# Token means and variances scaled on ScalarE instead of VectorE, with two steps of VectorE's order exchanged

## The reference, cut to what matters

```python
def _ln_c(v, eps=1e-06):          # over the 64 channels
    m = jnp.mean(v, axis=1, keepdims=True)
    s = jnp.var(v, axis=1, keepdims=True)
    return (v - m) / jnp.sqrt(s + eps)
...
# x is (4, 64, 128, 128)
x = x + window_attention(_ln_c(x))          # windows of 8x8, 4 heads of 16, with a position bias
t = _to_tokens(x)
# _ln_t: mean and variance over the last axis, eps 1e-5
t = t + moe(_ln_t(t))
x = _from_tokens(t, x)
...
def moe(x):
    router_probs = softmax(x @ router_w + router_b)      # 8 experts
    top_p, top_i = top_k(router_probs, 2)
    top_p = top_p / sum(top_p)
    expert_out = einsum('bnd,edc->bnec', x, expert_w) + expert_b
    return sum over the two of top_p * gathered expert_out
```

## Time and profile before

| | us |
|---|---|
| median of 3 runs | 1341.95 (1341.09 to 1342.88) |
| the profiled execution's own time | 1341.82 |
| its span, first to last instruction | 1340.0 |
| TensorE busy | 1237.9 (92%) |
| VectorE busy | 1138.4 (85%) |
| GpSimd busy | 918.0 (69%) |
| ScalarE busy | 875.7 (65%) |

### The profile page before, as it was taken

How to read it: one execution, slowest core, us unless ns; L and a number is a source line. 1 busy time by engine, 2 the same in 40 slices (tenths; PEclk the granted TensorE clock), 3 DMA queues, 4 the chain that set the end, 5 groups by cost and what they waited for, 6 DMA issues and landing times.

```text
span 1340.0 us, 47446 instructions
## 1 busy us (share of the span) xinstructions
PE 1237.9 (92%) x19840; PEld 781.4 (58%) x19840; DVE 1138.4 (85%) x2436; ACT 875.7 (65%) x1615; POOL 918.0 (69%) x809
## 2 busy tenths in 40 slices
PE   4579999999999999999999999999999999999986
PEld 3456666656666665665566566566566665666542
DVE  5548998998898899899888889989888888888865
ACT  5357677667666767767666777776667666666632
POOL 6456777777666777777766777876866667666642
PEclk8579999999999999999999999999999999999988
DMA  7012332322223233232222323322222222222221
GB/s 199 1 34 60 90 90 67 90 58 53 58 66 75 67 90 90 67 75 58 54 64 58 90 73 84 90 67 59 58 67 51 60 66 59 64 55 59 59 66 40
DMA packets 95554, 91.53 MB, mean 68 GB/s; under 512 B 26797, under 2 KB 62253, under 8 KB 95342
## 3 DMA queue, kind: packets, MB, share of 16 engines
q1 hardware_dynamic: 95342, 88.49, 27.0%
HBM read 36.03 MB, written 17.83 MB: 40 GB/s over the span
## 4 chain that ended last, share of the span: by engine, by line
PE 50%; DVE 23%; ACT 10%; issue 8%; POOL 7%; DMA 1%; SPq 1%; POOLq 0%; DVEq 0%; ACTq 0%
PE bank_y L523 10%; PE bank_s L407 8%; PE bank_s L381 6%; DVE t_g L950 6%; PE bank_t L422 5%; PE bank_o L435 4%; DVE mx L842 4%; DVE x L864 4%; PE bank_p L450 3%; PE bank_e L479 3%; ACT k_m L644 3%; PE bank_g L512 2%; DVE o_t L855 2%; ACT prob_t L668 2%; PE bank_e L472 2%
## 5 line engine op out<-in xcount | busy, mean ns | idle before, releaser
L1069 POOL TENSOR_TENSOR prob<-prob,mx 128x512 f32<-128x512 f32 x256 | 261.7, 1044 | 88.5 <-DVE mx L842 87.8
L523 PE MATMUL bank_y<-t_g,w_exp 128*64 128x512 f32 x1024 | 279.2, 622 | 16.7 <-DVE t_g L950 12.5
L664 ACT ACTIVATE prob<-prob 128x512 f32<-128x512 f32 x256 | 160.7, 628 | 147.4 <-POOL prob L1069 145.7
L1091 POOL TENSOR_TENSOR t_g<-t_t,g_copy 128x512 f32<-128x512 f32 x128 | 165.4, 1292 | 125.5 <-ACT g_copy L696 125.2
L668 ACT ACTIVATE prob_t<-bank_t 128x512 f32<-128x512 f32 x256 | 152.4, 595 | 135.8 <-PE bank_t L422 135.7
L1081 POOL TENSOR_TENSOR ln<-ln,mhalf 128x8 f32<-128x8 f32 x64 | 105.1, 1642 | 158.1 <-DVE ln L878 158.1
L835 DVE TENSOR_TENSOR prob<-bank_s,rel 128x1024 f32<-128x1024 f32 x128 | 156.6, 1223 | 39.7 <-PE bank_s L407 35.1
L422 PEld LDWEIGHTS bank_t<-idn,prob 128*128 128x128 f32 x1024 | 111.1, 144 | 130.2 <-issue 105.4
L422 PE MATMUL bank_t<-idn,prob 128*128 128x128 f32 x1024 | 169.1, 288 | 12.7 <-ACT prob_t L668 10.6
L950 DVE TENSOR_TENSOR t_g<-t_t,bank_p 128x512 f32<-128x512 f32 x256 | 174.3, 681 | 7.3 <-PE bank_p L512 6.9
L407 PEld LDWEIGHTS bank_s<-k_m,q_t 32*64 32x64 f32 x4096 | 114.0, 135 | 72.2 <-issue 68.6
(11 more groups left out here) (114 smaller groups left out, 2400.3 us busy)
## 6 DMA issues: line engine op xcount, KB each, us to landing
t_t<-t_rout SPq DMA_DIRECT2D x256, 128.0 KB, 2.4
x_in<-in_x SPq DMA_DIRECT2D x68, 256.0 KB, 3.3
r_b<-recip_rows SPq DMA_DIRECT2D x64, 256.0 KB
out_y<-y_out SPq DMA_DIRECT2D x128, 128.0 KB, 2.5
r_in<-sum_b SPq DMA_DIRECT2D x64, 16.0 KB
recip_rows<-r_out SPq DMA_DIRECT2D x64, 16.0 KB, 1.4
gate_sel<-in_sel SPq DMA_DIRECT2D x1, 512.0 KB
rel<-in_relb SPq DMA_DIRECT2D x1, 256.0 KB
```

Source lines behind the costliest of these rows:

```text
L523: mm(B_Y[C * a:C * a + C, :], w_exp[:, pair, :], t_g[:, (2 * pair + a) % TG, :], start=False, stop=(pair == MIXES // 2 - 1), skip_group_ch ...
L664: A(prob[:, i], prob[:, i], ACT.Exp).then_inc(p_ready.sem, 1)
L1069: G.tensor_tensor(sc, sc, mx[:, i, :].unsqueeze(2).broadcast_to([P, 2 * HEADS, NTOK]), ALU.subtract).then_inc(s_shifted.sem, 1)
L1091: G.tensor_tensor(t_g[:, u % TG, :], t_t[:, p, u % 2, :], g_copy[:, n % 2, :], ALU.mult).then_inc(tg_pool.sem, 1)
```

## The change

- The division of the token sums by 64 (L872) and the scaling of the summed squares with the epsilon (L878) leave VectorE. ScalarE does them as `Copy` with scale and bias, in two new functions `token_mean` and `token_variance`. They wait for VectorE's sums (`lsum`, `lvar`), and GpSimd now waits for them (`mean_ready`, `var_ready`). VectorE's sums go to rows 0 and 4 of `ln` in SBUF instead of to columns of the PSUM bank B_E.
- In ScalarE's slot `token_variance(j-2)` stands right behind `square(j-2)`, ahead of `copy_sums`; `token_mean(j-1)` stands between `exps(j+1, 0)` and `spread_values`.
- In VectorE's slot the second `maxima` goes ahead of `reciprocals` and of the statistics' steps (`reciprocals` ahead of two of them), and gate 7 ahead of `add_input`.

```diff
-        ln = sb("ln", [P, 4, ROWS])
+        ln = sb("ln", [P, 5, ROWS])
...
+            def token_mean(g):
+                act.wait_ge(lsum.sem, lsum.at(g, 1))
+                A(ln[:, 1, :], ln[:, 0, :], ACT.Copy, scale=1.0 / C).then_inc(mean_ready.sem, 1)
+
+            def token_variance(g):
+                act.wait_ge(lvar.sem, lvar.at(g, 1))
+                A(ln[:, 2, :], ln[:, 4, :], ACT.Copy, scale=1.0 / C, bias=LN_T_EPS).then_inc(var_ready.sem, 1)
...
# ScalarE's slot
                 if routing_on:
                     square(j - 2)
+                    token_variance(j - 2)
                 if outputting:
                     copy_sums(j - 1)
...
                 if projecting:
                     exps(j + 1, 0)
+                if outputting:
+                    token_mean(j - 1)
+                if projecting:
                     spread_values(j + 1, 1 - p)
                     exps(j + 1, 1)
...
# VectorE
             def token_mean(g, p):
                 dve.wait_ge(x2_ready.sem, x2_ready.at(g, 1))
-                V.tensor_reduce(B_E[:, LN_AT:LN_AT + ROWS], x2[:, p], AX.X, ALU.add).then_inc(lsum.sem, 1)
-                dve.wait_ge(lsum.sem, lsum.at(g, 1))
-                V.tensor_scalar(ln[:, 1, :], B_E[:, LN_AT:LN_AT + ROWS], 1.0 / C, None, ALU.mult).then_inc(lsum.sem, 1)
+                V.tensor_reduce(ln[:, 0, :], x2[:, p], AX.X, ALU.add).then_inc(lsum.sem, 1)
...
-                V.tensor_reduce(B_E[:, LN_AT + ROWS:LN_AT + 2 * ROWS], xc2[:, :, :], AX.X, ALU.add).then_inc(lvar.sem, 1)
-                dve.wait_ge(lvar.sem, lvar.at(g, 1))
-                V.tensor_scalar(ln[:, 2, :], B_E[:, LN_AT + ROWS:LN_AT + 2 * ROWS], 1.0 / C, LN_T_EPS, ALU.mult,
-                                ALU.add).then_inc(lvar.sem, 1)
+                V.tensor_reduce(ln[:, 4, :], xc2[:, :, :], AX.X, ALU.add).then_inc(lvar.sem, 1)
...
# VectorE's slot
                 if mixing:
                     routing(j - 3, 15, 19)
+                if attending:
+                    maxima(j, 1)
                 if work.step == SQUARES:
                     total_squares(work.batch)
+                if outputting:
+                    reciprocals(j - 1)
                 if work.step == PLANES:
                     total_planes(work.batch)
                 if work.step == SCALES:
                     turn_root(work.batch)
-                if outputting:
-                    reciprocals(j - 1)
-                if attending:
-                    maxima(j, 1)
...
+                if mixing:
+                    gate(j - 3, 1 - p, 7)
                 if outputting:
                     add_input(j - 1, 1 - p)
-                if mixing:
-                    gate(j - 3, 1 - p, 7)
-                if outputting:
                     token_mean(j - 1, 1 - p)
...
# GpSimd
-                pool.wait_ge(lsum.sem, lsum.at(g, 2))
+                pool.wait_ge(mean_ready.sem, mean_ready.at(g, 1))
...
-                pool.wait_ge(lvar.sem, lvar.at(g, 2))
+                pool.wait_ge(var_ready.sem, var_ready.at(g, 1))
```

More of the change, by code:

```diff
@@ L208, in build @@
         x2_ready = sem("x2_ready", primed=1)
-        lsum = sem("lsum", 2)
+        lsum = sem("lsum")
+        mean_ready = sem("mean_ready")
         xc_ready = sem("xc_ready")
         xc2_ready = sem("xc2_ready")
-        lvar = sem("lvar", 2)
+        lvar = sem("lvar")
+        var_ready = sem("var_ready")
         lrstd = sem("lrstd")
@@ L989, in slot @@
                     maxima(j + 1, 0)
-                if outputting:
-                    add_input(j - 1, 1 - p)
                 if mixing:
@@ L994, in slot @@
                 if outputting:
+                    add_input(j - 1, 1 - p)
                     token_mean(j - 1, 1 - p)
@@ L1135 @@
 ROUTE_AT = 64
-LN_AT = 448
 def rel_index():
```

## The result

The changed kernel takes **1381.28 us** (median of 4 runs, 1378.87 to 1382.69) against 1341.55 before: ratio 1.0293, 95% interval 1.0273 to 1.0312. Forecast were 1385 us, slower, with a range of 1362 to 1398. The profiled execution took 1382.69 us for a span of 1380.9.

The account below looks back on a forecast made before the run. The prediction took the loop from the input addition through t_n and L472 to gate 0 as the bound; 0.76 or 0.70 us a slot plus small terms summed to 43.3, so 1341.82 + 43.3 = 1385 us, range 1362 to 1398.

Parts of the forecast that it names:

- The loop over t_n: Each slot closes over input addition, mean, centring, square, variance, power, t_n, L472 and gate 0; a t_n delay counts in full.
- Part 1, the maxima: On VectorE the maxima cover the DMA's 0.92 us wait, but gate 0 waits for TensorE anyway: gain 0.
- Part 2, gate 7: On VectorE gate 7 starts at T+3.71, the sum ends at T+6.08 for T+5.70; TensorE's 0.14 us gap goes, gain 0.
- the first rival: Freed VectorE time counts: t_n keeps its place and TensorE gains 0.14 us a slot, 8 in all, 1334 us; chance 0.09.
- Part 3, the mean: ScalarE's mean copy waits for the sum: spreading at T+6.24, square at T+8.61, ending at T+9.23 for T+8.52.
- Part 4, the variance: Reduction waits for the square, ScalarE scales it: power at T+10.29, 0.76 us later; 0.70 in quiet slots; L488 stays covered.
- The sum: Over 62 slots, 27 with input work at 0.76 us, 30 quiet at 0.70, plus small terms: 43.3 us, giving 1385 us.
- the bound of 0.58: VectorE's two reductions, now writing another memory, take at least 0.58 us each; 0.69 was taken; 0.58 would give 1372.5 us.
- Freed VectorE time: The first rival: VectorE sheds 1.26 us a slot and a part gets through at gate 7's gap, 1334 us; chance 0.09.
- Half caught up: TensorE starts L472 sooner or the exponential is late already, leaving 0.2 to 0.5 us a slot: 1354 to 1371; chance 0.11.
- The clock: TensorE's clock gives way because it stands still twice a slot: 1402 us with a tenth of the slots; chance 0.06.
- The rival's worst case: Clock rival: products behind the stall at half clock in each slot, up to 3 us longer, 171 in all: 1550 us.

Follow-up runs that it names:

- e3: Kernel before with only the maxima moved ahead of the reciprocals and of the statistics' steps: 1342.15 us, ratio 0.9998.
- e2: Kernel before with gate 7 ahead of the addition as the only edit: 1348.35 us, ratio 1.0049.
- e4: Kernel before with only the mean's division moved to ScalarE: 1358.15 us, ratio 1.0126.
- e6: Changed kernel with the square moved ahead of the copy of the result on ScalarE: 1347.43 us, ratio 1.0034 to the kernel before.
- e11: Changed kernel with its mean copy moved behind the second exponential on ScalarE: 1387.5 us, ratio 1.0332 to the kernel before.
- e10: The same as e9 but without the exchange of gate 7: 1351.21 us, ratio 1.0066 to the kernel before.
- e7: Kernel before with maxima ahead of the reciprocals and, in slots with squares, the sum of squares ahead of gate 0: 1339.76 us, ratio 0.9976.
- e9: Kernel before with maxima before reciprocals, sum of squares before gate 0, gate 7 before addition, fewer router steps before second bias, square before result copy: 1335.27 us.

## Why the prediction was right

- **What bounds it.** The loop over t_n was read rightly: the delay of the power (0.73 in the slot with T = 521.81) is the delay of the token transposition (L472, now L474; 0.73) and nearly that of the next slot (20.72 for 20.01). In quiet slots 0.67 and 19.44 for 18.77. Forecast were 0.76 and 0.70 a slot.
- **Part 1, the maxima.** No gain in the middle, as put (e3). The step was incomplete at both ends. I priced neither the start, where VectorE's wait for the DMA was 4.28 us (the slot from 79.0 begins 2.3 us earlier, and 1.2 of them are left at the slot from 136.6), nor the move of the root's reciprocal behind the maxima and the sums' reciprocal: the slot from 643.59 takes 21.33 for 20.35 us, 0.98 more where 0.15 was put, because GpSimd's statistics of the next batch wait for that reciprocal, and its subtraction of the maxima, which ScalarE's exponential needs, stands behind them. Three such slots: 2.5 us. GpSimd and ScalarE in the slot from 643.59:

```profile
658.27 0.46 POOL L1034 TENSOR_TENSOR st<-st,rstd 128x128 f32<-128x128 f32 x1 [0.82 <-DVE rstd L840]
661.97 0.63 ACT L666 ACTIVATE prob<-prob 128x512 f32<-128x512 f32 x1 [2.11 <-POOL prob L1079]
```

- **Part 2, gate 7.** Times right to 0.01 us, and no gain from TensorE's gap, as put. The gap itself was sized too small: 0.14 us is the step from gate 7's end to the last experts, but without gate 7's delay the second scores come 0.35 us earlier (T+5.90 for T+6.25, in e2 and in the changed kernel). The 8 us of the first rival rest on that 0.14.
- **Part 3, the mean.** Spreading at T+6.24, square at T+8.61, both as worked out. e4, e6 and e11 show by runs that the cost runs through the operations between sum and square.
- **Part 4, the variance.** Power at T+10.26 for T+10.29 forecast. L488 (now L490) moved to T+11.61 and stayed covered, with 0.5 us to spare (the idle time of 0.49 ahead of L474) where the prediction gave it 0.2: the 0.62 us to the next transposition held a wait of 0.23 for ScalarE that is gone, and the step is 0.36 now. In e10 a late L488 costs by another way, through ScalarE's token copy, with L472 on time.
- **The sum.** 40 us for 43. The slots' share measured: from the fourth slot's start (136.6 before, 135.4 after) to the last one's (1300.3, 1337.5) 38.4 us are added; 42 were forecast. Errors of both signs meet in this. The three slots with the root add the 2.5 us of part 1. A delay of 0.73 and 0.67 where 0.76 and 0.70 were put takes off 1.5. And some thirteen slots of the kernel before were 0.15 to 0.8 us longer than their kind, such as the one of 20.79 us from 216.64, which takes 20.76 in the changed kernel: such slots show less delay or none, 4 us in all. I had priced all at the kind's usual length. The last stretch took 3.7 us longer in the profiled execution (43.4 for 39.7), where the prediction had put 1.0; TensorE was busy 3.0 us longer in it, at a mean clock of 0.78 for 0.88. The profiled execution is also the slowest of the four. So the slots' mechanism was right, and that the total came within 3 us is in part luck.
- **Bounds.** The reductions stayed at 0.69 us, so the bound of 0.58 was not needed. The estimate of 65 ns less for each, worked out from the Trainium skill's 60 ns in SBUF and 125 ns in PSUM ("Perfetto Trace Analysis", Optimizing Scalar/DVE Operations), does not show in the profiled duration: 0.69 before and after. The same section of the Trainium skill says that offloading some work to ScalarE may make sense where VectorE is saturated. It did not in this place: VectorE was busy over 90% of a slot before and still not what set its end, and e4 cost 16 us.
- **Rivals.** Freed VectorE time: no gain by itself, and e7 turns the 0.92 us a slot of the DMA's wait into only 2 us over the run. Half caught up: not seen. The clock: at full level in the middle, although TensorE stands still twice in each slot. (The rival's worst case adds up to 1556, not 1550.)

## What to carry to other kernels

Before a small operation is moved to a less busy engine, write down what stands behind it in that engine's queue and when its input is ready. Here two copies of 0.21 us cost 16 us and 2 us. The dear one had four instructions behind it and then the square, on which the slot hung; with one of the four taken out of that way (e6), 34 of the change's 40 us came back. Where several engines close one loop per iteration, an edit has no price of its own: the same exchange cost 21 us, cost 6.5 or gained 16, by what else was late; so look for the second-latest input at each meeting point and price edits together.

## What the runs showed that I had not expected

A wait can hide a second one of nearly the same end. VectorE's bias addition stood behind its own router steps and behind TensorE's scores within 0.2 us (e2), and TensorE's logits behind t_n and behind ScalarE's token copy, 0.20 us late in e9's quiet slots, where t_n starts at T+10.96 for T+11.31. On ScalarE the step from an exponential to the square was 0.53 us, to the copy of the result 0.65 (e6: 518.19 and the changed kernel: 550.64). The memory that is read does not explain it: in the kernel before, the step from an exponential to `g_copy`, which reads PSUM as the copy of the result does, was 0.52 us (526.73 to 527.25). What makes the copy of the result start later is open.
